# Causal attention in a six-layer decoder kernel: inverse totals and masked weights transposed together, then one fp32r matmul each for the tails and the spread

## What is computed

```python
kqv = (x @ Wqkv + bqkv).reshape(b, s, 3, 16, 32)
q, k, v = kqv[:, :, 0], kqv[:, :, 1], kqv[:, :, 2]
scores = jnp.einsum('bsnh,btnh->bnst', k, q) / math.sqrt(32)
scores = jnp.triu(scores) + -10000.0 * jnp.tril(ones, k=-1)
attn = jax.nn.softmax(scores, axis=2)
out = jnp.einsum('bnkq,bknh->bqnh', attn, v)
x = layernorm(x + out.reshape(b, s, 512) @ Wo + bo)
```

## Time and profile before

| what | before |
| --- | --- |
| median of 3 runs | 1682.01 us (1680.41 to 1682.33) |
| span of the profiled execution | 1681.9 us |
| PE matmul busy | 1576.0 us, 94% |
| PE weight loads | 1111.1 us, 66% |
| DVE busy | 1266.0 us, 75% |
| ACT busy | 949.4 us, 56% |
| POOL busy | 761.5 us, 45% |
| causal attention | from about 795 to 1240 us of the span |

### The profile page before, as it was taken

The page is one execution under the profiler, slowest core; times in us unless marked ns, Lnnn a source line. Parts: engine busy times, 40 slices in busy tenths (PEclk is TensorE's granted clock), DMA queues, the critical chain, the costliest instruction groups (busy, mean ns, idle before and its releaser), DMA issues. The chain is left out here.

```text
span 1681.9 us, 26408 instructions
## 1 busy us (share of the span) xinstructions
PE 1576.0 (94%) x8780; PEld 1111.1 (66%) x8812; DVE 1266.0 (75%) x2236; ACT 949.4 (56%) x1959; POOL 761.5 (45%) x728
## 2 busy tenths in 40 slices
PE   8999998999977999998999999999899999999995
PEld 5788875666634666666667566665557767777774
DVE  6467565778999999997686785876759899767573
ACT  3312225887876766766675474663635555555643
POOL 5043264778743445444532231231235257656564
PEclk9999999999998999999999999999899999999998
DMA  6200017543120000004221121221333100000000
GB/s 218 82 1 26 1 50 191 189 145 104 53 75 1 2 1 1 1 14 127 70 73 55 57 76 39 57 76 38 90 104 103 51 1 1 1 26 25 1 26 26
DMA packets 66850, 95.73 MB, mean 57 GB/s; under 512 B 12176, under 2 KB 28688, under 8 KB 66716
## 3 DMA queue, kind: packets, MB, share of 16 engines
q1 hardware_dynamic: 60044, 81.18, 15.8%
q0 software_dynamic: 6144, 12.60, 2.9%
q10 hardware_dynamic: 528, 0.26, 0.1%
HBM read 56.25 MB, written 4.19 MB: 36 GB/s over the span
## 5 line engine op out<-in xcount | busy, mean ns | idle before, releaser
L3159 PE MATMUL bank<-fp_xT,fp_weights_values 128*128 128x512 f32 x704 | 187.7, 403 | 7.5 <-DVE fp_gate L3053 5.2
L1919 ACT ACTIVATE causal_probs<-bank,causal_neg 128x512 f32<-128x512 f32 (+3 forms) x256 | 134.7, 532 | 104.4 <-DVE causal_neg L1989 70.4
L3159 PEld LDWEIGHTS bank<-fp_xT,fp_weights_values 128*128 128x128 f32 x704 | 128.2, 188 | 55.1 <-DVE fp_gate L3053 12.4
L3186 PE MATMUL bank<-fp_wd,fp_hT 128*128 128x512 f32 x528 | 133.8, 394 | 1.4 <-POOL fp_hT L2876 1.1
L3062 DVE SCALAR_TENSOR_TENSOR fp_up<-bank,fp_weights_scales,fp_up 128x512 f32<-128x512 f32 x132 | 99.1, 751 | 45.0 <-ACT fp_up L2945 37.6
L1199 POOL DMA_DIRECT2D causal_qS<-causal_qk x96 | 48.9, 516 | 163.1 <-DVE causal_qk L1191 163.1
L892 DVE TENSOR_REDUCE heads_neg<-bank 128x1 f32<-128x512 f32 x128 | 86.4, 677 | 43.2 <-PE bank L943 43.0
L3186 PEld LDWEIGHTS bank<-fp_wd,fp_hT 128*128 128x128 f32 x528 | 98.5, 188 | 25.8 <-issue 3.4
L1630 PE MATMUL bank<-weights_raw,ternary_qT 128*128 128x512 bf16 x432 | 104.0, 386 | 6.3 <-DVE ternary_z L1471 5.4
L1258 POOL TENSOR_TENSOR ternary_z<-ternary_z 128x1024 f32<-128x1024 f32 x16 | 38.8, 2425 | 152.5 <-DVE ternary_z L1471 143.3
L858 ACT ACTIVATE heads_probs<-bank,heads_neg 128x512 f32<-128x512 f32 x128 | 88.5, 697 | 34.3 <-DVE heads_neg L892 34.3
(11 more groups left out here) (284 smaller groups left out, 4250.6 us busy)
## 6 DMA issues: line engine op xcount, KB each, us to landing
pairs_xd<-X SPq DMA_DIRECT2D x64, 128.0 KB, 2.6
pairs_cd<-in_ctx SPq DMA_DIRECT2D x64, 128.0 KB, 2.7
causal_qS<-causal_qk SPq DMA_DIRECT2D x96, 64.0 KB, 2.8
causal_qS<-causal_qk POOLq DMA_DIRECT2D x96, 64.0 KB, 2.5
causal_kS<-causal_qk SPq DMA_DIRECT2D x96, 64.0 KB, 2.7
causal_kS<-causal_qk POOLq DMA_DIRECT2D x96, 64.0 KB, 2.5
X<-in_x SPq DMA_DIRECT2D x4, 1024.0 KB, 8.0
heads_cT<-in_ctxT SPq DMA_DIRECT2D x4, 1024.0 KB, 6.0
```

Source lines behind the costliest of these rows:

```text
L1919: act.activation(probs_of(i)[:, h + one], view[:, one], ACT.Exp, bias=neg[:, G % 2, at:at + 1], accum_out=total[:, G % 2, at:at + 1]).then ...
L3159: last = pe.matmul(banks[4 + g][:], values[:, g, n % NI, of], xT[:, part, g], start=part == 0, stop=part == 1)
L3186: last = pe.matmul(banks[t][:], hT[:, n % SLOTS, a, t * P:(t + 1) * P], wd[:, c, i], start=i == 0 and k == 0, stop=i == NI - 1 and k == 2)
```

## The change

The inverses and the masked weights go into one tile `cols` of 4 blocks of 128 (+4) columns. In it the 12 weights stand in columns 0 to 11 and the 16 inverses in columns 16 to 31, and both are repeated in four groups of 32 columns. One PE step transposes the four blocks (`turn_columns`), so partitions 0 to 31, 32 to 63, 64 to 95 and 96 to 127 of the result hold the same numbers. ACT copies all of it rounded to fp32r (`col_highs`), DVE overwrites partitions 64 to 127 with the rest of the rounding (`col_lows`). The tails are made the same way: the sums of the values come out on 128 rows, DVE masks them into `spread` (used as a scratch tile), ACT rounds them (`tail_highs`), and DVE writes the rest into partitions 32 to 63 and 96 to 127 (`tail_lows`). One fp32r matmul over 128 partitions then adds high x high, high x low, low x high and low x low. The spread becomes one fp32r matmul of a 0/1 table `of_head` by the same transposed columns. The turn now also waits for the reciprocal, the reciprocal and the weights wait for the previous group's turn, and `keep_spread` waits for the tails' low parts. Three tables are loaded instead of two, a larger tile is cleared by POOL, and the program is built with half of the default room for the descriptors of POOL's DMAs.

```diff
-        mask, lowest, neg, total, weight = first.mask, first.lowest, first.neg, first.total, first.weight
-        count, extra, inverse, v_column, wT = first.count, first.extra, first.inverse, first.v_column, first.weightT
-        step_in = first.step_in
+        mask, lowest, neg, total = first.mask, first.lowest, first.neg, first.total
+        count, extra, v_column = first.count, first.extra, first.v_column
+        step_in = m.sbuf("step_in", [P, NT - 1, P])
+        own, of_head = m.sbuf("own", [P, P]), m.sbuf("of_head", [P, P], F32R)
+        cols, colsT = m.sbuf("cols", [P, NT * (P + GH)]), m.sbuf("colsT", [P, S], F32R)
...
-        tails_own = m.sbuf("tails_own", [64, D])
-        tails, own = tails_own[0:LATER], tails_own[32:32 + LATER]
+        tails = m.sbuf("tails", [P, D], F32R)
...
-        v_ready, v_kept, sums_ready, tails_kept = (m.sem(n) for n in ("v_ready", "v_kept", "sums_ready", "tails_kept"))
+        v_ready, v_kept, sums_ready, tails_ready, tails_high, tails_kept = (
+            m.sem(n) for n in ("v_ready", "v_kept", "sums_ready", "tails_ready", "tails_high", "tails_kept"))
...
-        weights_ready, counted, wholed, inverted, spread_ready, spread_kept = (
-            m.sem(n) for n in ("weights_ready", "counted", "wholed", "inverted", "spread_ready", "spread_kept"))
+        weights_ready, counted, wholed, inverted, cols_high, spread_ready, spread_kept = (
+            m.sem(n) for n in ("weights_ready", "counted", "wholed", "inverted", "cols_high", "spread_ready", "spread_kept"))
...
+        table_ready = m.sem("table_ready")
...
-        padded = weight[:, 0:(NT - 1) * LATER].rearrange("p (i c) -> p i c", c=LATER)
-        own_columns = weight[:].rearrange("p (i c) -> p i c", c=LATER + GH)[:, :, 0:GH]
+        shifted = cols[:].rearrange("p (i c) -> p i c", c=P + GH)[:, :, 0:P].rearrange("p i (a r) -> p i a r", a=4)
+        own_columns, inverse_columns = shifted[:, 0:NT - 1, :, 0:GH], shifted[:, :, :, 16:16 + GH]
...
             for i in range(NT):
...
-            pool.memset(weight[:], 0.0).then_inc(counts, 1)
+            pool.memset(cols[:], 0.0).then_inc(counts, 1)
...
             def own_weights(G):
...
-                act.activation(own_columns, by_tile(neg[:, G % 2, later_tiles]), ACT.Exp,
-                               bias=lowest[:, 0:1]).then_inc(weights_ready, 1)
+                act.wait_ge(p_turned, G * NU)
+                act.activation(own_columns, by_tile(neg[:, G % 2, later_tiles]).unsqueeze(2).to_broadcast([P, NT - 1, 4, GH]),
+                               ACT.Exp, bias=lowest[:, 0:1]).then_inc(weights_ready, 1)
+            def col_highs(G):
+                act.wait_ge(p_turned, (G + 1) * NU)
+                act.wait_ge(spread_ready, G)
+                act.activation(colsT[:], banks[3 + ((G + 1) * NU - 1) % 2][:], ACT.Copy).then_inc(cols_high, 1)
+            def tail_highs(b):
+                act.wait_ge(tails_ready, b + 1)
+                act.activation(tails[:], spread[:], ACT.Copy).then_inc(tails_high, 1)
...
             def keep_spread(G):
+                act.wait_ge(tails_kept, 2 * (G // NF + 1))
...
                 for f in range(NF):
...
+                if G >= 1 and k == TURN[NU - 1] + 1 - STEPS:
+                    col_highs(G - 1)
...
+                if g == 1 and k == SUMS + 1 and G < GROUPS:
+                    tail_highs(b)
...
+                if n == 8:
+                    act.wait_ge(consts, 16 * 5)
+                    act.activation(of_head[:], oT[:, 0, 0:P], ACT.Copy).then_inc(table_ready, 1)
                 for t in range(NT):
...
-                dve.tensor_tensor(by_tile(extra[:, later_tiles]), own_columns, by_tile(count[:, later_tiles]),
+                dve.tensor_tensor(by_tile(extra[:, later_tiles]), own_columns[:, :, 0], by_tile(count[:, later_tiles]),
...
-                if G >= 1:
-                    dve.wait_ge(spread_ready, G)
-                dve.reciprocal(inverse[:], old).then_inc(inverted, 1)
+                dve.wait_ge(p_turned, G * NU)
+                dve.reciprocal(inverse_columns, by_tile(old).unsqueeze(2).to_broadcast([P, NT, 4, GH])).then_inc(inverted, 1)
...
             def keep_bias():
...
-            def keep_weights(G):
-                dve.wait_ge(p_turned, (G + 1) * NU)
-                dve.wait_ge(o_ready, G)
-                dve.tensor_copy(wT[0:LATER], banks[3 + ((G + 1) * NU - 1) % 2][0:LATER, 0:(NT - 1) * P]).then_inc(kept_by_dve, 1)
+            def col_lows(G):
+                dve.wait_ge(cols_high, G + 1)
+                dve.tensor_tensor(colsT[64:P], banks[3 + ((G + 1) * NU - 1) % 2][64:P], colsT[64:P].bitcast(F32),
+                                  ALU.subtract).then_inc(kept_by_dve, 1)
...
             def keep_tails(b):
...
-                dve.tensor_tensor(tails, banks[5][0:LATER], own, ALU.mult).then_inc(tails_kept, 1)
+                dve.tensor_tensor(spread[:].rearrange("p (g c) -> p g c", g=NF), banks[5][:].rearrange("p (g c) -> p g c", g=NF),
+                                  own[:].unsqueeze(1).to_broadcast([P, NF, P]), ALU.mult).then_inc(tails_ready, 1)
+            def tail_lows(b):
+                dve.wait_ge(tails_high, b + 1)
+                for at in (slice(32, 64), slice(96, P)):
+                    dve.tensor_tensor(tails[at], spread[at], tails[at].bitcast(F32), ALU.subtract).then_inc(tails_kept, 1)
...
             def add_output(b, t):
...
+                if g == 1 and k == SUMS + 2 and G < GROUPS:
+                    tail_lows(b)
                 for f in range(NF):
...
-                        keep_weights(G - 1)
+                        col_lows(G - 1)
...
                 for j in range(NT - 1):
-                    last = pe.matmul(banks[5][0:LATER], step_in[:, j], v[:, j + 1], start=j == 0, stop=j == NT - 2)
+                    last = pe.matmul(banks[5][:], step_in[:, j], v[:, j + 1], start=j == 0, stop=j == NT - 2)
...
             def score(n):
...
-            def turn_weights(G):
+            def turn_columns(G):
...
+                pe.wait_ge(inverted, G + 1)
...
-                for i in range(NT - 1):
-                    last = pe.transpose(banks[3 + n % 2][0:LATER, i * P:(i + 1) * P], padded[:, i], ident)
+                for i in range(NT):
+                    last = pe.transpose(banks[3 + n % 2][:, i * P:(i + 1) * P], cols[:, i * P:(i + 1) * P], ident)
...
             def values(G):
...
-                pe.wait_ge(tails_kept, b + 1)
+                pe.wait_ge(tails_ready, b + 1)
...
             def tail(G):
...
-                pe.matmul(banks[5][:, 0:(NT - 1) * P], tails[:, g * P:(g + 1) * P], wT[0:LATER], start=False, stop=True,
+                pe.wait_ge(tails_kept, 2 * (G // NF + 1))
+                pe.matmul(banks[5][:, 0:(NT - 1) * P], tails[:, g * P:(g + 1) * P], colsT[:, 0:(NT - 1) * P], start=False, stop=True,
...
             def spread_inverse(G):
-                pe.wait_ge(inverted, G + 1)
+                if G == 0:
+                    pe.wait_ge(table_ready, 1)
...
-                for i in range(NT):
-                    for h in range(GH):
-                        one = inverse[:, i * GH + h:i * GH + h + 1].to_broadcast([P, DH])
-                        last = pe.matmul(banks[7][DH * h:DH * h + DH, i * P:(i + 1) * P], one, ident, start=True, stop=True)
-                last.then_inc(spread_ready, 1)
+                pe.matmul(banks[7][:], of_head[:], colsT[:], start=True, stop=True).then_inc(spread_ready, 1)
...
 def causal_tables():
...
-    later, own_head = np.zeros((P, NT - 1, P), np.float32), np.zeros((P, D), np.float32)
-    for i in range(NT - 1):
+    later, own_head, inverse_head = np.zeros((P, NT - 1, P), np.float32), np.zeros((P, P), np.float32), np.zeros((P, P), np.float32)
+    for i in range(NT):
         for h in range(4):
-            later[:, i:, i * 4 + h] = 1
-            own_head[i * 4 + h] = np.arange(D) // 32 % 4 == h
-    return later, own_head
+            for quadrant in range(0, P, 32):
+                if i < NT - 1:
+                    later[:, i:, quadrant + i * 4 + h] = 1
+                    own_head[quadrant + i * 4 + h] = np.arange(P) // 32 == h
+                if quadrant in (0, 64):
+                    inverse_head[quadrant + 16 + i * 4 + h] = np.arange(P) // 32 == h
+    return later, own_head, inverse_head
...
 def lay_out(a):
...
-    later, own_head = causal_tables()
+    later, own_head, inverse_head = causal_tables()
...
-    nc = Bacc("TRN2", target_bir_lowering=False, num_devices=1)
+    nc = Bacc("TRN2", target_bir_lowering=False, num_devices=1, dynamic_dma_scratch_size=8192)
...
```

17 lines of the change are left out of this document (7 added, 10 removed).

## The result

| what | before | after |
| --- | --- | --- |
| median of 20 runs each | 1682.73 us (1680.41 to 1685.68) | 1685.47 us (1683.13 to 1688.35) |
| after over before | | 1.0016, 95% interval 1.001 to 1.0022 |
| profiled execution | span 1681.9 us | span 1681.5 us, time 1683.35 us |
| PE matmul busy | 1576.0 us | 1559.0 us |
| DVE busy | 1266.0 us | 1280.1 us |

The account below looks back on a forecast made before the run. TensorE was taken to bound one stretch per batch, mostly VectorE the other three groups. Terms 1.53 + 0.78 - 0.80 - 1.80 gave -0.3 us; with +1.4 for the clock, +1.1 on 1681.9: 1683.0 us, range 1674 to 1690.

Parts of the forecast that it names:

- PE, per group: TensorE's work in each group: tail saves 0.84 us, spread saves 0.96, turn adds 0.11; 1.69 less in all.
- DVE, per group: VectorE's work in each group: low-column subtraction adds 0.14 us over the old copy, longer reciprocal adds 0.36.
- A: First-group spread to the previous batch's last output tile's end: +0.51 us each in batches 1 to 3, +0.78 in batch 0.
- B, C, D: The three intervals after A, spread to spread: -0.20 us in each B, -0.80 in all; C and D taken as 0.
- The end: After the last spread the engines wait on one another, so tail and spread savings both count: -1.80 us.
- The clock: Behind spreads, where TensorE idles: two more falls to 1.2 GHz in nine steady intervals, +1.4 us.
- Rival 3: The clock falls in nearly every B, C and D: ten falls at 0.7 us, 1688.6 us. Chance 0.17.
- Rival 1: TensorE bounds everywhere, so its saving counts in all 16 groups: 27 us less, 1655 us. Chance 0.08.
- Rival 2: The tails' low parts find cover in A and TensorE's savings count whole: 8.1 us less, 1675 us. Chance 0.16.
- Rival 4: VectorE pays more for the reciprocal and the tails' low parts: 3.3 us more, 1686 us. Chance 0.09.
- Rival 6: The fp32r matmuls of tail and spread don't run in one pass: 1688 us. Chance 0.02.
- Rival 5: No further fall of the clock, as the skill page's rule gives: 1681.6 us. Chance 0.15.

Follow-up runs that it names:

- the old spread: The changed kernel with the spread back in 16 matmuls and a reciprocal of 16 outputs; 1686.74 us, ratio 1.0021.
- the fourfold spread: The changed kernel with the spread's matmul issued four times in the first three groups of each batch; 1685.66 us, ratio 1.0013.
- the tails early: The changed kernel with the two low-tail subtractions issued ahead of the last output tile's addition; 1684.34 us, ratio 1.0006.
- filled in all groups: The kernel before with unused matmuls in waits of the last two groups and ahead of first scores in batches 0 to 2; 1687.01 us, ratio 1.002.
- both early, fourfold spread: The changed kernel with low tails and low columns subtracted before the addition, reciprocal halved, spread issued four times in three groups a batch; 1681.42 us, ratio 0.999.
- the same, filled: The kernel of both early, fourfold spread, with unused matmuls in nine steps of the last two groups; 1678.15 us, ratio 0.997.
- both early with half the reciprocal: The changed kernel with low tails and low columns subtracted ahead of the addition and a reciprocal of 32 outputs; 1681.25 us, ratio 0.999.
- filled in the last groups: The kernel of both early with half the reciprocal, plus unused matmuls in nine steps of the last two groups; 1680.9 us, ratio 0.9985.

## Why the prediction was right, and where it was not

The forecast of 1683.0 us and its range of 1674 to 1690 hold the 1685.47 us, and a change of under 0.2% is what came. Of the 2.5 us between forecast and result 0.7 is the kernel before, which 20 runs put at 1682.73 and three at 1682.01. Its total was right partly by errors of opposite sign, and that part is luck.

**PE, per group: right in kind, 0.18 too much.** Tail 0.26 instead of 0.17, spread 0.32 instead of 0.23, turn 0.36, gaps gone. The saving is 1.51 us a group instead of 1.69. PE's busy time fell by 17.0 where some 20 was named, with more of it at half clock.

**DVE, per group.** Reciprocal +0.30, where 0.36 was taken. By the figures of the Trainium skill (VectorE: DVE Perf Modes, "First, the fixed hardware budget") the prediction estimated 0.40; the measurement decides. The step from the low columns to what follows went from 0.47 to 0.72, +0.25 where 0.14 was taken. DVE's busy time rose by 14.1 (named: 13).

**The tails' subtractions: mis-sized.** 2 x 0.70 = 1.40 in place of 2 x 0.61 = 1.22; the 0.61 is the time from the start of the addition to that of the copy, which started before the addition had ended, and the addition's own time in that row is 0.69. One of 32 x 512 took 685 ns, as one of 128 x 512 does.

**A: the sum's step that failed.** The prediction had PE's -0.85 up to the addition and DVE's +1.36 behind it, with the tail's saving lost. Measured for batch 1: from the spread to the addition 39.25 us against 40.27, -1.02; from the addition to the next mask 3.97 against 2.15, +1.82; from the mask to the spread 2.39 against 3.10, -0.71, as the tail's shorter matmul does count there. Sum +0.09, not +0.51; the three batches gave +0.09, +0.31 and -0.04. Batch 0's first interval gave +0.53 where +0.78 was taken.

**B, C, D.** C was +0.31, +0.31 and +0.14, D +0.09 three times. For D the step held: the wait of 0.54 that was to cover DVE's added time is gone in after, though the cover was not whole: the old spread's short reciprocal gave 0.28 back in D. C has no such wait, and there it gave 0.27 back. "C and D within 0.5" stood. B of batches 0 and 1 without a fall would be about 0.1 shorter, not 0.20 (20.70 with the fourfold spread against 20.84).

**The end.** From the last spread to the output 1.86 instead of 2.53 us, -0.67. The last three intervals together were 1.1 shorter, with 3.4 us more at half clock than before; with the tails early, where they had the same, 2.2 shorter. -1.80 was taken for the tail and the spread together.

**The clock: right that it falls more often, wrong in what a fall costs, by a misread row.** Two more falls at 0.7 us were taken. The profile has five more, and over the runs it is some eight. The 0.7 was the difference of two B in the kernel before, 22.77 us with a fall against 22.07 without one. Compared instruction by instruction, 0.60 of it is there 0.7 us behind the spread, 4.6 us before the clock fell, and it is a wait of DVE for POOL: in batch 2 POOL issued four DMAs just when DVE's variance was ready, and made the norm's factors behind them.

```profile
1055.41 1.97 POOL L1199 DMA_DIRECT2D causal_kS<-causal_qk  x4 [2.93 <-issue]
1057.39 1.04 POOL L164 TENSOR_TENSOR norm_rstd<-norm_var_eps,norm_power 128x4 f32<-128x4 f32 x1
1058.47 0.55 DVE L158 TENSOR_SCALAR X<-X,norm_mean_var,norm_rstd 128x512 f32<-128x512 f32 x1 [0.57 <-POOL norm_rstd L164]
```

The kernel before, filled in all groups (the last run above), settles it. Its batch 1 and batch 2 both had full clock in B, the same wait of 0.57 us stands in batch 2, and batch 2 is 0.6 longer:

```profile
951.00:973.08 22.08, 20.54 (x163) 14.76 (x162) 18.89 (x44) 15.17 (x46) 5.93 (x12) 1.00 0.25 71
1061.58:1084.27 22.69, 20.93 (x163) 14.75 (x162) 19.26 (x44) 15.16 (x46) 6.15 (x13) 1.00 0.24 68
```

So that fall cost 0.1 at most. In after DVE comes to this instruction later, by the subtractions, and doesn't wait: batch 2's B is 0.62 shorter than before, a gain that the prediction did not have.

What a fall costs depends on where it lies. Two kernels that differ only in the filling of the last groups had the same instructions in batch 0's B, one with 3.4 us at half clock (both early, fourfold spread) and one with none (the same, filled):

```profile
843.29:865.28 21.99, 20.04 (x132) 15.45 (x131) 17.61 (x41) 15.42 (x47) 5.89 (x12) 0.92 0.22 64
842.68:863.38 20.70, 18.57 (x133) 14.13 (x131) 17.53 (x41) 15.21 (x47) 5.89 (x12) 1.00 0.24 67
```

That is 1.3 us for one fall, and after had just this one (21.99), which is 1.3 of the profiled stage's balance. In batch 1's B one stretch of 3.4 us left 21.97 and one of 6.8 made it 23.39, in two kernels with the same instructions up to there (both early with half the reciprocal, unfilled and filled in the last groups); a second stretch of 3.4 cost 0.37 (22.34 in after, 21.97 with the fourfold spread). In D a fall cost 0.6 to 1.5, as PE at half clock becomes the bound; in after D had none.

The stage can be summed as if no interval had more half clock than before, with the values of other traces where after had a fall (B from the fourfold spread's, the last batch from that and the tails-early one): +0.5 for batch 0's A, +0.4 for the other three, +0.75 for C, +0.3 for D, -1.0 for the B of batches 0 to 2 (the wait for POOL with them) and -2.4 for the last batch's intervals from its B on, together -1.5 us, where the prediction's sum had -0.3. The profiled stage took +1.8, so 3.3 us went with 20 us more at half clock, 0.16 for each; and over the runs 2.7 + 1.5 = 4.2 with 27 us more, 0.16 as well. This is an estimate. Over the runs of before alone, longer times go with more half clock at 0.19 to 0.25 us for each us, over those of after at 0.10.

**The rivals.** Rival 3 (slower, from about five falls on) comes nearest: there were five more falls, though in B alone and not in C and D, and at 0.16 for each us one of 3.4 us costs an estimated 0.55 and not 0.7. The time came out between the forecast and its 1688.6. Rival 1 fell: C and D are longer, and the one B that is clearly shorter is so by 0.62. Rival 2 fell for this kernel (no cover: the subtractions follow one another without a gap), and the cover that it spoke of was one line away: the wait of 2.03 us ahead of the addition, of which the 1.4 us of subtractions left 0.60. Rival 4's mechanism is there, but not its size. Rival 6 fell by the rows of the two matmuls. Rival 5 fell: PE never waited longer than 1.81 us between 832 and 1190 us, and the clock fell five more times. The Trainium skill (TensorE: Matmul & The Clock Gate, "Why this matters for your kernels") asks only that idle gaps stay under some 3 us. By that rule none of the six places would be there. The same page of the Trainium skill, under "A second HAM failure mode: psum-queue depth-cycling", tells of a kernel whose frequent micro-idles between groups of matmuls made the clock swing between its two levels. With that the trace agrees: PE busy 1.60 of 3.41 us in pieces, then 0.50.

## What to carry to other kernels

Where engines hand over to one another, work taken off TensorE is worth what its stretch of the trace says, and then the clock asks for part of it back: taking three quarters of the spread away gained 3.5 us in some intervals and nothing in the kernel. Before new VectorE work is put into a hand-written order, look for the wait that it could stand in; here the same two subtractions cost 1.4 to 1.8 us behind an addition that they didn't cost ahead of it. When timing a change of one or two thousandths, compare the mean granted clock of the runs too, and ask in which interval the half-clock stretches lie, not only how many there are. And before the difference of two twin intervals is put down to the clock, find the first instruction at which they part: here it stood ahead of the fall.

## What the runs showed of the hardware

- The same instructions with and without one 3.4 us stretch at 1.2 GHz: 20.79 against 19.33 us in a D where PE is nearly the bound (17.89 of 19.33 busy), and 21.99 against 20.70 in batch 0's B. In batch 1's B, 21.97 us with one stretch of 3.4 us and 23.39 with one of 6.8.
- Two stretches of 6.8 us in the last two groups cost 1.7 us in one pair of kernels and 0.7 in another.
- Less TensorE work gave more time at half clock: 52 to 69 us a run for a spread of 4 instead of 16 matmuls, 51 to 78 for the whole change, 61 with the old spread put back. Moving the tails' subtractions left it near 80.
- A VectorE subtraction of 32 x 512 took 685 ns and one of 64 x 512 694 ns, as long as one of 128 x 512 (692): the number of partitions made no difference.
- A reciprocal of 128 x 64 took 553 ns and one of 128 x 16 253 ns, 6.3 ns for each added output of a partition.
- POOL held VectorE up: four DMA issues took it 1.97 us, and the norm's factors, made behind them, kept VectorE waiting 0.57 us.
